# Second attention of a two-layer kernel: each chunk of 128 tokens in two halves of 64, with a state between them

## The reference, cut to what matters

```
def step(carry, qkv):
    S_K, C_QV, G = carry
    q_t, k_t, v_t = qkv
    C_prev = GAMMA * C_QV
    k_C = jnp.einsum('bhk,bhkv->bhv', k_t, C_prev)
    G = GAMMA * G + k_t[..., :, None] * k_C[..., None, :]
    S_K = GAMMA * S_K + k_t[..., :, None] * k_t[..., None, :]
    C_QV = C_prev + q_t[..., :, None] * v_t[..., None, :]
    S_C = jnp.einsum('bhij,bhjv->bhiv', S_K, C_QV)
    o_t = jnp.einsum('bhk,bhkv->bhv', q_t, S_C - G)
    return ((S_K, C_QV, G), o_t)
_, outs = jax.lax.scan(step, (S_K0, C_QV0, G0), (q, k, v))
out = outs.transpose(1, 0, 2, 3).reshape(Bs, Ts, H * DV)
return out @ Wo
```

## Time and profile before

| | us |
|---|---|
| median of 3 runs | 700.54 (699.94 to 701.98) |
| span of the profiled execution | 697.8 |
| TensorE busy | 640.0 (92%) |
| VectorE busy | 421.9 (60%) |
| ScalarE busy | 301.7 (43%) |
| GpSimd busy | 254.2 (36%) |

### The profile page before, as it was taken

The page is one execution under the profiler, slowest core; times in us unless marked ns, Lnnn a source line. Parts: engine busy times, 40 slices in busy tenths (PEclk is TensorE's granted clock), DMA queues, the critical chain, the costliest instruction groups (busy, mean ns, idle before and its releaser), DMA issues.

```text
span 697.8 us, 26323 instructions
## 1 busy us (share of the span) xinstructions
PE 640.0 (92%) x10918; PEld 545.8 (78%) x10918; DVE 421.9 (60%) x1384; ACT 301.7 (43%) x1017; POOL 254.2 (36%) x387
## 2 busy tenths in 40 slices
PE   5799999888759969999999999999997999999995
PEld 4466666666649957888888888888875899998995
DVE  3777677867534326577777686868674454444443
ACT  1556466543025404555545454545442353333231
POOL 2366566555620031122525252524242332232225
PEclk9789999998869989999999999999999899999999
DMA  7999000000048300000000000000401567676472
GB/s 195 310 323 268 22 3 3 2 10 17 24 137 243 87 26 7 8 8 8 20 11 18 16 15 15 16 20 8 156 15 24 170 208 233 215 232 227 144 241 61
DMA packets 50486, 65.68 MB, mean 94 GB/s; under 512 B 5169, under 2 KB 40209, under 8 KB 47425
## 3 DMA queue, kind: packets, MB, share of 16 engines
q1 hardware_dynamic: 44992, 57.22, 26.6%
q0 software_dynamic: 2912, 6.03, 2.6%
q10 hardware_dynamic: 2464, 0.76, 0.5%
HBM read 49.45 MB, written 18.87 MB: 98 GB/s over the span
## 4 chain that ended last, share of the span: by engine, by line
PE 58%; DVE 2%; another core or an unknown queue 1%; DMA 1%; issue 1%; ACT 0%; SPq 0%; DVEq 0%; PEldq 0%
PE bank L1903 6%; PE quad L1761 6%; PE quad L1885 6%; PE quad L1887 6%; PE bank L1786 4%; PE pair L1723 4%; PE bank L1809 3%; PE quad L1767 2%; PE pair L1724 2%; PE pair L1725 2%; PE bank L1819 2%; PE bank L1822 2%; PE pair L1748 2%; PE bank L1812 2%; PE bank L1905 1%; PE quad L1890 1%
## 5 line engine op out<-in xcount | busy, mean ns | idle before, releaser
L2159 DVE TENSOR_TENSOR h_masked<-quad,const 128x1536 f32<-128x1536 f32 (+2 forms) x66 | 112.7, 1707 | 63.6 <-PE quad L1767 54.4
L1997 ACT ACTIVATE f_sa<-quad 128x256 f32<-128x256 f32 (+1 forms) x115 | 40.1, 351 | 94.2 <-PE quad L1887 76.8
L2273 DVE TENSOR_TENSOR f_hid<-f_sa,quad 128x256 f32<-128x256 f32 (+1 forms) x115 | 43.0, 379 | 53.0 <-ACT f_sa L1997 52.2
L2377 POOL DMA_INDIRECT moe_slots<-g_pay,g_slot x28 | 28.9, 1031 | 77.3 <-PE bank L1831 68.8
L1885 PE MATMUL quad<-f_xT,wall 128*128 128x256 f32 (+1 forms) x190 | 51.5, 354 | 3.7 <-DVE f_hid L2273 3.6
L1903 PE MATMUL bank<-wall,f_hid 128*128 128x128 f32 x390 | 50.7, 277 | 1.1 <-DVE f_hid L2276 0.9
L1903 PEld LDWEIGHTS bank<-wall,f_hid 128*128 128x128 f32 x390 | 47.8, 192 | 3.7 <-DVE f_hid L2276 2.8
L1887 PE MATMUL quad<-f_xT,wall 128*128 128x256 f32 (+1 forms) x190 | 50.4, 347 | 0.0
L1761 PE MATMUL quad<-h_qk 32*128 32x128 f32 x1024 | 47.0, 298 | 0.0
L1974 ACT ACTIVATE h_gT<-bank 128x128 f32<-128x128 f32 x64 | 17.7, 277 | 66.1 <-PE bank L1812 66.1
L1761 PEld LDWEIGHTS quad<-h_qk 32*128 32x128 f32 x1024 | 34.7, 187 | 9.3 <-issue 7.4
(11 more groups left out here) (412 smaller groups left out, 1785.8 us busy)
## 6 DMA issues: line engine op xcount, KB each, us to landing
wall<-moe_w SPq DMA_DIRECT2D x23, 1088.0 KB, 5.2
moe_slots<-blank SPq DMA_DIRECT2D x2, 2112.0 KB, 25.9
wall<-in_experts_dram SPq DMA_DIRECT2D x1, 4120.0 KB, 22.1
e_w<-in_experts_dram SPq DMA_DIRECT2D x15, 257.5 KB, 3.1
moe_slots<-blank SPq DMA_DIRECT2D x1, 1984.0 KB, 9.8
moe_slots<-e_yg SPq DMA_DIRECT2D x7, 256.0 KB, 3.7
f_xg<-moe_slots SPq DMA_DIRECT2D x12, 132.0 KB, 4.6
moe_w<-in_moe_w_dram SPq DMA_DIRECT2D x1, 1408.0 KB, 7.2
```

The lines of the kernel that those rows point to most:

```text
L1997: act.activation(sa[g % 3][:, 0:s], up_bank(n, f)[:, 0:s], ACT.Silu).then_inc(f_sa, 1)
L2159: dve.tensor_tensor(masked[k % 4][:, :, a * P:z * P], quad[:, :, a * P:z * P], cst("causal")[:, None, a * P:z * P].to_broadcast([P, HPG, ( ...
L2273: dve.tensor_tensor(hid[n % 2][:, f, 0:s], sa[g % 3][:, 0:s], up_bank(n, f)[:, T1:T1 + s], ALU.mult)\
L2377: pool.indirect_dma_start(out=t["moe1_slots"], out_offset=bass.IndirectOffsetOnAxis(ap=slot[:, b * 2 + k:b * 2 + k + 1], axis=0), in_=pay[ ...
```

## The change

Each chunk is split in two halves of 64 tokens. The products of `products` are made for each half alone, 64 x 64, with the two halves on different column tiles of the array (`tile_position=(h * D, r * S)`); the mask and `masked` shrink to 64 columns a part. Between the halves stands a state `mids`, the chunk's state plus the sums of its first half, in four buffers. Every product with a state takes the chunk's state for the first half and `mids` for the second. The chunk products go in two calls, `chunk_first` and `chunk_second`, around `from_states`, and in each `left` works on one half's rows while `right` works on the other's. The sums for a state are made for each half: those of the first half of the next unit and of gT of the unit before go to `right`, those of a second half to `left`. VectorE adds the first to the state (`mids`, two additions, after aT), and the new state comes from `mids` and `left`. `banks_free` waits for these reads before the banks are written again, `s_first` keeps `chunk_second` behind `chunk_first`, and oT waits for the additions. kg's two parts change places, kqt is scaled by a column instead of a constant, and the expert count moves to the bank `token`.

```diff
+HL_SUB = 64
-    parts["causal"] = np.concatenate([row <= col, row < col, row <= col], axis=1)
+    early, late = row % HL_SUB, np.arange(HL_SUB)[None, :]
+    parts["causal"] = np.concatenate([early <= late, early < late, early <= late], axis=1)
+    parts["decay_half"] = np.where(row < HL_SUB, 1.0, GAMMA ** P)
+        S = HL_SUB
-        masked = [sb(f"h_masked{k}", [P, HPG, 3 * P]) for k in range(4)]
+        masked = [sb(f"h_masked{k}", [P, HPG, 3 * S]) for k in range(4)]
+        mids = [sb(f"h_mid{k}", [P, 3 * D]) for k in range(4)]
+        def half(r):
+            return slice(r * S, (r + 1) * S)
@@ tensor
-            pe.sem_inc(s_gc, 1)
-            pe.sem_inc(s_oc, 3)
-            pe.sem_inc(s_ac, 1)
@@ token_major
-                    pe.wait_ge(s_oc, now + 1)
+                    pe.wait_ge(s_oc, now - 2)
+                    if (i, k) == (CHUNKS - 1, PER + 2):
+                        pe.wait_ge(s_tab, 1)
@@ products
                     for a in range(2):
-                        for h in H:
-                            last = pe.matmul(quad[:, h, a * P:(a + 1) * P], qk[q][head(h), 1 - a, :],
-                                             qk[q][head(h), a, :], start=True, stop=True, tile_position=(h * D, 0))
+                        for r in range(2):
+                            for h in H:
+                                last = pe.matmul(quad[half(r), h, a * S:(a + 1) * S], qk[q][head(h), 1 - a, half(r)],
+                                                 qk[q][head(h), a, half(r)], start=True, stop=True,
+                                                 tile_position=(h * D, r * S))
...
+            def banks_free(i, k):
                 now = i * PER + k
-                pe.wait_ge(s_gc, upto(now + 1, UNITS + 1))
-                pe.wait_ge(s_ac, upto(now + 1, UNITS + 1))
-                pe.wait_ge(s_oc, now + 1)
-                pe.wait_ge(s_st, upto(now + 6, UNITS))
+                if now >= 0:
+                    pe.wait_ge(s_midkv, upto(now + 1, UNITS))
+                if now >= 2:
+                    pe.wait_ge(s_midg, now - 1)
+                if now >= 3:
+                    pe.wait_ge(s_oc, now - 2)
+                    pe.wait_ge(s_st, upto(now - 2, LAST))
...
+            def chunk_left(i, k, r, part, first):
+                new = masked[(k - 1) % 4]
+                for h in H:
+                    k_op = kg[k][half(r), 1, head(h)] if part else vt[k][half(r), head(h)]
+                    last = pe.matmul(left[head(h), part * P + r * S:part * P + (r + 1) * S], k_op,
+                                     new[half(r), h, 0:S] if part else new[half(r), h, S:2 * S], start=first,
+                                     stop=True, tile_position=(r * S, h * D), skip_group_check=True)
+                return last
...
+            def chunk_first(i, k):
+                for part in range(2):
+                    if live(i, k, 0):
+                        last = chunk_left(i, k, 0, part, part == 0)
+                    if live(i, k, -2):
+                        last = chunk_right(i, k, 1, part, part == 0)
...
             def from_states(i, k):
                 for part in range(2):
+                    for r in range(2):
+                        if live(i, k, 0):
+                            for h in H:
+                                of = mids[now % 4] if r else states[k]
+                                pe.matmul(left[head(h), part * P + r * S:part * P + (r + 1) * S],
+                                          of[head(h), D:2 * D] if part else of[head(h), 2 * D:3 * D],
+                                          qk[k][head(h), 1 - part, half(r)], start=False, stop=True,
+                                          tile_position=(h * D, h * D), skip_group_check=True)
...
+            def chunk_second(i, k):
+                if now >= 0:
+                    pe.wait_ge(s_first, now + 1)
+                if near:
+                    pe.wait_ge(s_kqt, (now + 3) * 2)
+                elif far:
+                    pe.wait_ge(s_ng, now + 3)
+                pe.nop(nofuse=True)
+                for part in range(2):
+                    if live(i, k, 0):
+                        last_left = chunk_left(i, k, 1, part, False)
+                    if live(i, k, -2):
+                        last_right = chunk_right(i, k, 0, part, False)
+                if near:
+                    for h in H:
+                        last_right = pe.matmul(right[head(h), P + D:P + 2 * D], kqt[n][half(0), 0, head(h)],
+                                               kg[n][half(0), 1, head(h)], start=not live(i, k, -2), stop=True,
+                                               tile_position=(0, h * D), skip_group_check=True)
+                if done:
+                    for h in H:
+                        last_left = pe.matmul(left[head(h), 2 * P:2 * P + 2 * D], kqt[q][half(1), 0, head(h)],
+                                              kg[q][half(1), :, head(h)], start=False, stop=True,
+                                              tile_position=(S, h * D), skip_group_check=True)
...
+                if last_left is not None:
+                    last_left.then_inc(s_left, 1)
+                if far:
+                    if near:
+                        pe.wait_ge(s_ng, now + 3)
+                    for h in H:
+                        last_right = pe.matmul(right[head(h), P:P + D], kqt[m][half(0), 0, head(h)],
+                                               kg[m][half(0), 0, head(h)], start=False, stop=True,
+                                               tile_position=(0, h * D), skip_group_check=True)
+                last_right.then_inc(s_right, 1)
@@ scalar
-                                   scale=GAMMA ** P).then_inc(s_kqt, 1)
+                                   scale=cst("decay_half")[:, 0:1]).then_inc(s_kqt, 1)
-                    act.wait_ge(s_right, now - 1)
+                    act.wait_ge(s_right, now + 2)
+                    act.wait_ge(s_midkv, upto(now + 2, UNITS))
+                    act.wait_ge(s_midg, upto(now, UNITS))
                     act.activation(oT[q][:, :], right[:, 0:P], ACT.Copy).then_inc(s_oc, 1)
@@ vector
-                    dve.wait_ge(s_left, now)
-                    dve.wait_ge(s_gc, now + 1)
+                    dve.wait_ge(s_gc, now)
                     dve.tensor_tensor(aT[q][:, :], left[:, P:2 * P], cst("decay_row"), ALU.mult).then_inc(s_ac, 1)
-                if live(i, k, -3):
-                    dve.wait_ge(s_right, now - 2)
-                    dve.wait_ge(s_oc, now + 1)
+                if live(i, k, 0) or live(i, k, -2):
+                    dve.wait_ge(s_right, now + 1)
+                if live(i, k, 0):
+                    dve.tensor_tensor(mids[now % 4][:, D:3 * D], states[k][:, D:3 * D], right[:, P + D:P + 3 * D],
+                                      ALU.add).then_inc(s_midkv, 1)
+                if live(i, k, -2):
+                    q = unit(i, k, -2)[1]
+                    dve.tensor_tensor(mids[(now - 2) % 4][:, 0:D], states[q][:, 0:D], right[:, P:P + D], ALU.add)\
+                        .then_inc(s_midg, 1)
-                    dve.scalar_tensor_tensor(out=states[q][:, :], in0=states[q][:, :], scalar=GAMMA ** P,
-                                             in1=right[:, P:P + 3 * D], op0=ALU.mult, op1=ALU.add).then_inc(s_st, 1)
+                    dve.scalar_tensor_tensor(out=states[q][:, :], in0=mids[(now - 3) % 4][:, :], scalar=GAMMA ** P,
+                                             in1=left[:, 2 * P:2 * P + 3 * D], op0=ALU.mult, op1=ALU.add)\
+                        .then_inc(s_st, 1)
@@ gpsimd
-                pool.wait_ge(s_right, i * PER + k - 1)
+                pool.wait_ge(s_right, i * PER + k + 2)
```

More of the change, by code:

```diff
@@ new lines, in chunk_right @@
+            def chunk_right(i, k, r, part, first):
+                new, old = masked[(k - 1) % 4], masked[(k - 3) % 4]
+                q = unit(i, k, -2)[1]
+                for h in H:
+                    k_op = kg[q][half(r), 0, head(h)] if part else vt[q][half(r), head(h)]
+                    last = pe.matmul(right[head(beside(h)), half(r)], k_op,
+                                     old[half(r), h, 0:S] if part else new[half(r), h, 2 * S:3 * S], start=first,
+                                     stop=True, tile_position=(r * S, beside(h) * D), skip_group_check=True)
+                return last
@@ L1782, in from_states @@
+            def chunk_first(i, k):
[5 more added lines that the diff above has]
+                if live(i, k, 0) or live(i, k, -2):
+                    last.then_inc(s_first, 1)
+            def from_states(i, k):
+                now = i * PER + k
                 q = unit(i, k, -2)[1]
@@ L1783, in from_states @@
                 for part in range(2):
-                    if live(i, k, 0):
[L1785 to L1789, removed]
-                    if live(i, k, -2):
[L1791 to L1795, removed]
+                    for r in range(2):
```

(16 more changed lines are left out.)

83 lines of the change are left out of this document (38 added, 45 removed).

## The result

The changed kernel takes 880.29 us (median of 4 runs, 874.04 to 886.68), the kernel before 700.24: ratio 1.257 (95% interval 1.249 to 1.265). The profiled execution took 874.04 us, its span is 871.9. Forecast were 822 us and a range up to 860: the sign and the mechanism held, the size did not, and the time lies outside the range.

The account below looks back on a forecast made before the run. Bound taken: TensorE, its instructions supplied in blocks by DMA queue 8. Terms 121 + 4 - 2.8 - 0.4 = +122 us on the 697.8 us span, about 820, plus 2.7 to the median: 822 us; range 725 to 860.

Parts of the forecast that it names:

- What bounds it: Second attention: TensorE's instructions come by queue 8 through two buffers, so a block cannot take less than one turn.
- More instructions: Second attention: 226 pairs a unit instead of 114, 1.79 blocks a unit, so 111 blocks instead of 56.
- Its price: Second attention: 111 blocks at a turn of 3.4 us are 377 us, 121 more than 256; stage ends +4.
- Less TensorE work: Scores, chunk products, sums and one more change of form: -0.53 us a unit, bringing nothing under the supply.
- Rival A: Supply is not the bound and the halves pay: -22 us, 675 us; chance 0.11.
- rival D: A floor for each pair in the stage, at 21 ns 4.75 us a unit: 739 us; chance 0.03.
- New waits at 0: TensorE and ScalarE's oT newly wait for the additions in each step: 0, since the supply ends later.
- VectorE: Mask multiply 0.95 us, two additions 0.2 and 0.25; gains 0.35 us a unit off the path: nothing.
- The end: After the second attention, VectorE's table no longer waits for the last oT, so f_hid ends earlier: -2.8 us.
- The dropped increments: Three semaphore increments dropped before the first projection: at most 0.7 us, taken as -0.4.
- If the clock falls, above 855: Sign to watch: if TensorE's clock falls in the gaps, the time is above 855 us.

Follow-up runs that it names:

- the burst: Kernel before plus 1280 products of 4 columns on 32x32 tiles in one single step (chunk 4, unit 4): 778.0 us, ratio 1.110.
- the added narrow products: Kernel before plus 28 or 56 products of 4 columns on 32x32 tiles in each step: 774.1 us (ratio 1.103) and 909.4 us (ratio 1.296).
- The fewer-product kernel: Changed kernel with all waits, banks and additions but fewer products, 138 pairs a unit instead of 226; does not compute the layer: 719.4 us, ratio 1.027.
- five other profiles: Kernel before with halved state products, with 28 or 56 narrow products, with 4 wide products, and the burst: 5.80 or 5.81 us at this place.
- the end alone: Kernel before, but in the last chunk VectorE no longer waits for oT and the right bank: 698.79 us against 701.14, ratio 0.9958.
- the second profile: The changed kernel run once more, unaltered, for a second profile: 872.3 us, ratio 1.247 against the kernel before.
- the kernel with halved products: Kernel before with each state product of 128 columns made in two of 64, same tiles and waits: 721.9 us, ratio 1.032.

## Why the prediction was right, and where it was wrong

*What bounds it* held: queue 8, two buffers, one block a turn. The block edges in the burst (128 + 128 instructions to the record), the added narrow products and the changed kernel's stops all show it, and in no profile do two transfers of queue 8 start less than 3.2 us apart. The fewer-product kernel shows that all the waits of the change together cost at most some 20 us.

*More instructions* held: 111 blocks forecast and found, 18,086 records for 18,100.

*Its price* is the step that failed. I took 3.4 us a turn, below both whole turns that the trace of before had (3.7 and 3.5), since the DMA engines would be quiet. The turns of the changed kernel average 3.90: 111 x 0.5 = 55 us, which is the whole miss (52 of span). Of the 0.5, 0.4 is the turn itself (median 3.81): in the 90 turns with a stop (of the matmuls or of the weight loads) a transfer was usable 2.52 us after its start and the next started 1.40 us after that, with DMA engines at a share of 0.05. At a share of 1.18 the stop at 71.09 had read 2.5 as well, and only one turn in the rush at 653.45, share 0.99, reads longer, 6.56: usable 2.67 after its start, but the next transfer started only 3.9 after that. So quiet DMA engines gave no discount that shows between these. The other 0.1 is the long turns, 20 of 111 above 4.2 us, 15.5 us over a turn of 3.8 together: six with an output projection at a clock of 0.71 or less (5.3 us), the one in the rush (2.8), and thirteen others, seven of them at 0.95 and more, for which the trace names no reason. The range failed with it, since its upper end, 860, was made of turns of 3.7 and nothing above. Why real work gives 3.8 where the burst gives 3.65, and 2.52 to the use where the burst gives 2.40, is open.

*Less TensorE work* was wrong too, though under the supply it cost nothing. The pieces by their starts at full clock, where no stop cuts them (us a unit):

| | before | forecast | after |
|---|---|---|---|
| scores | 0.88 | 0.55 | 0.71 |
| state products | 0.60 | 0.60 | 0.78 |
| chunk products | 0.90 | 0.46 | 0.38 + 0.29 |
| state sums | 0.29 | 0.37 | 0.51 |
| projections and turns | 1.19 | 1.19 | 1.19 |
| sum | 3.86 | 3.33 (with one change of form) | 3.86 |

The -0.53 us a unit became nothing. I had scaled each group by its columns; a pair costs some 9 ns with four columns, 10 with 64 (0.62/64 in the state products, without the change of form) and 14 with 128 (0.44/32), so halving the columns and doubling the pairs gains little or loses. Rival A, priced at 675 us, had no such gain to reach (this is read from pieces; a whole stage of halves with the supply out of the way wasn't run), and rival D was right in kind, a floor for each pair, but at 9 ns and not 21. The 25 ns of the Trainium skill (TensorE: Matmul & The Clock Gate, section "Wait — 56ns, not 53.3ns?") don't show here for products on different tiles: 9 to 14 ns.

*New waits at 0* held in the changed kernel (1.1 us); with fewer instructions they would be 8. *VectorE* held: the mask multiply 0.958 us for 0.95, the two additions 0.39 together for 0.45. *The end*, -2.8, took the late oT of one profile for the rule: 1.6 us is what the dropped wait gives against five other profiles. That the times of the end alone say 2.4 to 2.9 is within their noise. *The dropped increments*, -0.4: the idle time before the first projection is 1.27 us for 1.97, but the projection starts 1.5 later (1.98 in the second profile, and up to 5.9 later in the kernels made from the one before), so the term can't be told from what differs between profiles. *If the clock falls, above 855* held as a sign, but 8 to 11 us are all that the sort gives the clock; most of the miss is the turn.

## What to carry to other kernels

Count TensorE's instructions as well as its columns: here a block of 256 (128 pairs of load and matmul, so 64 fp32 products) was never had in less than 3.2 us and on average came every 3.65 to 3.9, and by these numbers a loop that already uses a block each 4.6 us has room for about a fifth more (4.57/3.8), an estimate and an upper end: with 28% more, the kernel with halved products already stopped for some 8 us. A split that halves columns and doubles products pays only while both sums stay under the limit, and price the limit by the whole turns that a trace shows, not by a discount that no row shows. Where blocks differ, add up the longer of turn and work block by block, with the work at the clock that the stops leave.

## What was not expected of the hardware

A matmul with four columns on a 32 x 32 tile cost 9 ns a pair in a row of 56 at full clock, and one with 64 columns 10. In the burst queue 8's turns came as short as 3.4 us and as long as 4.1 with nothing else changed. The one turn beside full DMA engines (share 0.99, 357 GB/s) took 6.56 us, and the same place in the second profile 6.51 (share 1.00, 358 GB/s); in the first, 3.9 us of it lay between TensorE's restart and the next transfer's start.
